# Scores of the two longest row blocks moved ahead of the product with v, in a three-stage attention pipeline on one core

## The reference

```python
def _L0_attn_ref(x, w_q, w_kv, w_dense):      # x: layer norm of (8, 512, 256)
    q = jnp.einsum('bsh,he->bse', x, w_q).reshape(b, sq, GROUPS, HPG, KVC)   # 4 groups, 4 heads each, width 128
    kv = jnp.einsum('bsh,he->bse', x, w_kv)
    k, v = jnp.split(kv, 2, axis=-1)           # one k and one v for each group
    ...
    scores = jnp.einsum('bqgpd,bkgd->bgqpk', q, k) * (SCALE / LAYER_INDEX)
    ...
    scores = jnp.where(causal[None, None, :, None, :], scores, -jnp.inf)
    probs = jax.nn.softmax(scores, axis=-1).astype(x.dtype)
    ctx = jnp.einsum('bgqpk,bkgd->bqgpd', probs, v).reshape(b, sq, HEADS * KVC)
    return jnp.einsum('bse,eh->bsh', ctx, w_dense)
...
x = x + 0.5 * ffn(layernorm(x)); x = x + attn(layernorm(x)); x = x + 0.5 * ffn(layernorm(x))
```

## Time and profile before

| | |
|---|---|
| time, 3 runs | 2637.43, 2638.76, 2639.93 us (median 2638.76) |
| the profiled execution | 2639.36 us, of which its span is 2637.5 us and 1.86 us lie around it |
| PE busy | 2536.8 us, 96% of the span |
| DVE busy | 2157.0 us, 82% |
| ACT, POOL busy | 946.0 us (36%), 910.4 us (35%) |
| one item of the attention, 984.50 to 1104.30 us | 119.80 us, PE busy 117.75, DVE 101.47, ACT 90.65, POOL 47.01, granted clock 1.00 |

### The profile page before, as it was taken

The page is one execution under the profiler, slowest core; times in us unless marked ns, Lnnn a source line. Parts: engine busy times, 40 slices in busy tenths (PEclk is TensorE's granted clock), DMA queues, the critical chain, the costliest instruction groups (busy, mean ns, idle before and its releaser), DMA issues. The chain is left out here.

```text
span 2637.5 us, 45987 instructions
## 1 busy us (share of the span) xinstructions
PE 2536.8 (96%) x14500; PEld 2341.1 (89%) x14500; DVE 2157.0 (82%) x6164; ACT 946.0 (36%) x2546; POOL 910.4 (35%) x1952
## 2 busy tenths in 40 slices
PE   6999999999996999999999999997999999999998
PEld 6999999999995889898888988896899999999997
DVE  6888888888886788888888888886888888888887
ACT  3111101111113677777777777774211011111100
POOL 4332333233224334343434343333423333332321
PEclk9999999999998999999999999998999999999999
DMA  6000000000001454554455455555100000000000
GB/s 192 9 1 1 1 1 1 1 1 1 1 27 56 81 91 91 89 89 84 91 91 88 83 93 88 89 90 121 51 1 9 9 1 9 9 9 1 9 9 9
DMA packets 378738, 117.30 MB, mean 44 GB/s; under 512 B 338560, under 2 KB 377472, under 8 KB 378496
## 3 DMA queue, kind: packets, MB, share of 16 engines
q1 hardware_dynamic: 378496, 114.36, 22.1%
HBM read 26.24 MB, written 4.19 MB: 12 GB/s over the span
## 5 line engine op out<-in xcount | busy, mean ns | idle before, releaser
L555 PE MATMUL ffn_ring<-ffn_mix_weights,ffn_yT 128*128 128x384 f32 x5760 | 1154.9, 341 | 8.1 <-DVE ffn_mix_weights L790 5.8
L555 PEld LDWEIGHTS ffn_ring<-ffn_mix_weights,ffn_yT 128*128 128x128 f32 x5760 | 1007.1, 189 | 58.5 <-DVE ffn_mix_sums L725 15.7
L727 DVE SCALAR_TENSOR_TENSOR ffn_mix_sums<-ffn_ring,ffn_w,ffn_mix_sums 128x384 f32<-128x384 f32 x896 | 550.4, 615 | 241.5 <-PE ffn_ring L555 224.8
L1579 POOL CAST attn_probsT<-attn_turned 128x1024 fp32r<-128x1024 f16 (+3 forms) x512 | 348.5, 723 | 508.1 <-DVE attn_probs L1444 496.9
L605 PE MATMUL ffn_ring<-ffn_out_weights,ffn_avT 128*128 128x512 f32 x1536 | 440.4, 397 | 7.0 <-POOL ffn_avT L1028 4.5
L1512 ACT ACTIVATE attn_exponentials<-attn_exponentials,attn_score_neg_max 128x512 f32<-128x512 f32 (+3 forms) x512 | 285.6, 558 | 169.8 <-DVE attn_score_neg_max L1427 169.6
L605 PEld LDWEIGHTS ffn_ring<-ffn_out_weights,ffn_avT 128*128 128x128 f32 x1536 | 281.2, 188 | 36.2 <-POOL ffn_avT L1028 5.7
L1273 PE MATMUL attn_ctx<-attn_probsT,attn_v 128*128 128x256 f32 (+2 forms) x1536 | 276.1, 329 | 14.9 <-issue 7.8
L1273 PEld LDWEIGHTS attn_ctx<-attn_probsT,attn_v 128*128 128x128 f32 x1536 | 242.1, 190 | 37.3 <-issue 9.3
L1444 DVE SCALAR_TENSOR_TENSOR attn_probs<-attn_exponentials,attn_prob_factor,attn_probs 128x512 f16<-128x512 f32 (+3 forms) x512 | 254.3, 558 | 22.0 <-ACT attn_probs L1521 21.3
L1521 ACT ACTIVATE attn_probs<-attn_exponentials,attn_prob_factor 128x512 f16<-128x512 f32 (+3 forms) x512 | 250.1, 552 | 27.5 <-DVE attn_prob_factor L1437 16.0
(11 more groups left out here) (141 smaller groups left out, 2858.8 us busy)
## 6 DMA issues: line engine op xcount, KB each, us to landing
ffn_mix_stage<-in_L_ffn_q_proj_dram SPq DMA_DIRECT2D x32, 128.0 KB, 2.5
ffn_mix_stage<-in_L_ffn_k_proj_dram SPq DMA_DIRECT2D x32, 128.0 KB, 2.5
ffn_mix_stage<-in_L_ffn_v_proj_dram SPq DMA_DIRECT2D x32, 128.0 KB, 2.9
ffn_out_stage<-in_L_ffn_o_proj_dram SPq DMA_DIRECT2D x16, 256.0 KB, 3.0
attn_turned<-attn_probs SPq DMA_TRANSPOSE x256, 4.0
out_dram<-x SPq DMA_DIRECT2D x8, 512.0 KB, 2.9
x<-in_L_attn_x_dram SPq DMA_DIRECT2D x7, 512.0 KB, 8.1
early_stage<-in_L_attn_w_q_dram SPq DMA_DIRECT2D x4, 512.0 KB, 5.3
```

Of the source, the lines that this page charges most:

```text
L555: last = pe.matmul(bank[:, 0:QKV], yT[:, t % 2, h, k * P:(k + 1) * P], mix_half(e, wh)[:, k], start=(n == 0), stop=(n == 3 * CK - 1))
L727: dve.scalar_tensor_tensor(into, bank[:, 0:QKV], w[:, t, e:e + 1], into, ALU.mult, ALU.add).then_inc(mix_done, 1)
L1579: pool.tensor_copy(cast(i), landed(n, i).rearrange("p (j h q) -> p j h q", h=HL, q=P)).then_inc(t_cast, 1)
```

## The change

Two moves, one on PE and one on DVE. On PE, `scores(now, 3)` and `scores(now, 2)` come ahead of `attend(last)` in a slot. On DVE, `score_max(now, 2)` comes ahead of `split_context(last)`. No instruction is added, removed or altered. The lists of ACT, POOL and SP are as they were.

```diff
@@ -1357,11 +1357,11 @@
-                if last:
-                    attend(last)
                 if now:
                     scores(now, 3)
                     scores(now, 2)
+                if last:
+                    attend(last)
                 place("B")
@@ -1472,10 +1472,10 @@
                 if now:
                     score_max(now, 3)
+                    score_max(now, 2)
                 if last:
                     split_context(last)
                 if now:
-                    score_max(now, 2)
                     score_max(now, 1)
                     score_max(now, 0)
```

## The result

| | before | changed |
|---|---|---|
| median (6 runs each) | 2638.79 us | 2659.93 us |
| lowest to highest | 2637.43 to 2640.27 | 2655.45 to 2662.16 |
| span of the profiled execution | 2637.5 us | 2657.4 us (its own time 2659.2) |
| PE busy | 2536.8 us | 2547.1 us |
| one item of the attention | 119.80 us | 122.68 us |

The ratio is 1.0077 (95% interval 1.0066 to 1.0088): the changed kernel is 0.8% slower, 21.1 us, against 21 us in the forecast. The spans differ by 19.9 us.

What follows compares the result with a forecast made beforehand. PE, 96% busy, was taken to bound the kernel, with about 2 us idle per item. Terms summed to +2.8 us per item: 16.6 for six middle items, +2.0 first, +2.4 last, together +21, hence 2660 us, range 2643 to 2676.

Steps and rivals of the forecast that it cites:

- Scores 3 wait for q: Plain slots: scores 3 wait for q's low half, making each 7.07 us; four take 28.3 against 27.0, +1.3 us per item.
- k of group 0: Projected last in slot 15; scores 3 of the next item's slot 0 wait out its whole split, +1.67 us per item.
- k in slots 7 and 11: Scores 3 of the next slot wait for k's low half and restart, 0.26 us each; +0.45 us per item.
- Slots 2 and 3: Scores 3 and 2 fill attend's wait for v, but DVE behind add_to_x delays k's low half: -0.3 us per item.
- Slot 14: The second z transpose's wait of 0.35 us for q's low half goes: -0.35 us per item.
- The DVE move: Maximum 2 ahead of split_context: ACT gets it earlier, filling only idle time; dense still starts unhindered; costs nothing, 0.2 us to spare.
- the forecast's aside: In the slot after the v slots, the wait for q hides a further wait, of dense for attend's low half.
- dense is not the bound: Rival judged: dense becomes the bound, waiting for attend's low half in v slots too; +16 us on top, 2676 us; chance 0.10.
- The granted clock: Rival: PE's idle gaps bring the clock down, attend and scores costing 3 us more per item; 2681 us; chance 0.04.
- No change: Rival: waits for q only replace those for the casts, gains and losses cancel within 5 us; 2641 us; chance 0.10.
- Faster: Rival: q's low half comes at least 0.5 us earlier, by 6.44 us into the slot; 2632 us; chance 0.08.
- the wait row for q: Sign of being right: PE scores waiting for DVE attn_qT, near 0.4 us each in some 30 to 40 slots.

Runs made afterwards that it cites:

- S = 9 to 14: Kernel before with both moves made only in slots 9 to 14, the light ones: 2648.79 us, ratio 1.0044.
- added DVE instruction: One more DVE sum into a scratch tile ahead of q's low half: 2686.84 us in the changed kernel, 2643.32 us in the kernel with the DVE move alone.
- Slot 0 alone: Kernel before with both moves made only in slot 0 of each item: 2649.4 us, ratio 1.004.
- Slot 3 alone: Kernel before with both moves made only in slot 3 of each item: 2629.47 us, ratio 0.9965.
- The earlier k: Changed kernel with slot 15's two projections of the next item, q and k, one place earlier: 2642.65 us, ratio 1.0013.

## Why the prediction was right, and where it was not

Counted in both traces from the start of slot 0 of an item to that of the next (of the last item, to the first attend behind it), the loss is spread over the items as the forecast had it:

| | forecast | measured |
|---|---|---|
| first item | +2.0 us | 129.22 - 127.46 = +1.8 |
| six middle items | +16.6 | 736.65 - 720.43 = +16.2 |
| last item | +2.4 | 117.88 - 115.83 = +2.1 |

Together that is 20.0 us, and the spans differ by 19.9. That the median fell within 0.1 us of the forecast is luck, since the changed kernel's own runs spread over 7 us.

*Scores 3 wait for q.* Right in place and size. Forecast 7.07 us for a plain slot and 28.3 for the four, measured 7.13 and 7.07 for slots 9 and 10 and 14.12 for 12 and 13, 28.3 in all. The light slots alone (S = 9 to 14) cost 9.3 us, and an added DVE instruction went through to PE in full in the plain slots.

*k of group 0.* Right: slot 15 went from 8.87 to 10.50 us, and slot 0, where the restart falls, from 7.20 to 7.27, together +1.70 where 1.67 was forecast. Slot 0 alone cost 10.75 us.

*k in slots 7 and 11.* Right: slot 7 went from 7.91 to 8.13 us where 0.26 was forecast, and slot 11 is 8.26 us where 8.01 + 0.2 was the sum. In both, scores 3 of the next slot start 0.10 us behind the end of k's low half.

*Slots 2 and 3.* Right in the sum: 1121.08 - 1104.53 = 16.55 us against 17.01, with 0.1 of restart behind it, where -0.3 was forecast. The reason given, that DVE is late with k's low half behind add_to_x, is borne out by the timeline of DVE, in which no row from the first of these two to the second has idle time in brackets:

```profile
1113.35 1.27 DVE L1459 TENSOR_TENSOR x<-x,attn_dense 128x512 f32<-128x512 f32 x2
...
1120.29 0.69 DVE L1412 TENSOR_TENSOR attn_kT<-attn_projections,attn_kT 128x512 fp32r<-128x512 f32 x1
```

No run takes add_to_x away, so its own share is not shown. Slot 3 alone, followed by an attend that covers k's split, keeps 9.2 us. In the changed kernel much of that goes to the wait for k (0.42 in slot 4's row).

*Slot 14.* Right in size: 1202.15 - 1194.66 = 7.49 us against 7.90, where -0.35 was forecast. It doesn't need both moves. The wait of the second z transpose is gone with either half alone, and slot 14 then lasts 7.66 us (PE half) or 7.39 (DVE half, as part of its 0.8 us per item).

*The DVE move.* This is the step that failed, though the number held. I wrote that maximum 2 earlier "only fills idle time" and costs nothing. It is worth 6.7 us alone and 14 us inside the change (2674.09 against 2659.93). Nor is it free for dense, which waits 0.3 us for attend's low half in slot 9. I had priced its direct neighbours, dense and exponential 2, and not followed the queue on ACT one step on: exponential 2, then the high half of q, then q's low half, which is what scores 3 wait for. The forecast was still right, and in this part by luck, because the 6.92 us that it was built on hold only with this move (7.03 in the changed kernel, with the restart of 0.10 in it that the sum books by itself; 7.16 without the move). I had read them from a slot in which attend came early, and assumed that they did not depend on where attend stands. On PE they don't; through DVE and ACT they do, and the second half of the change happens to undo that.

*The rivals.* Dense waits 2.8 us in all, in slot 9 of seven items and once in slot 10; slot 9 is the one that the forecast's aside named, and dense is not the bound. The granted clock stayed at 1.00 over the stretch from 1100 to 1222 us, with the idle 1.46 us in it. "No change" needed the wait for q at under half, and the four plain slots cost 1.3 us together, as forecast. "Faster" needed q's low half 0.5 us earlier, and DVE's 0.57 us of idle in front of maximum 1 shows why it couldn't be. Of the signs named ahead, the wait row for q has 22 entries of 0.33 us on average, and not 30 to 40 of 0.4; by the starts there are five such slots per item, and the view doesn't list them all.

Two misses among the experiments can be read from the traces. The earlier k gave 17.3 us and not 14.3: slot 15 became shorter by about 2.27 us and not by 2.05 in each of seven items, and slot 3 of the first item by 0.8, 16.5 us over the attention. Why slot 15 gives 0.2 us more than its two waits is not settled. The added instruction cost 26.9 us and not 31: the plain slots grew by 0.3 us and the slots 1, 5 and 6 by 0.25, but slots 7 and 11, which wait for k and not for q, by only 0.21 and 0.08 where 0.34 was expected. What is left in both lies within the spread of the changed kernel's own runs (2655.45 to 2662.16).

## What to carry to other kernels

A product whose inputs were ready long ago is cover: placed between the last split of an operand and the first use of it, it hides the latency of two engines. Moving it away costs, in each round, what nothing else covers of that latency, even with PE 96% busy: here about 0.3 us in a plain slot, 1.7 where k came last, and next to nothing in the slots with a v projection. Before moving a step up, look at when its newest operand is finished, counted from the start of the round, and at which engine that moment is tied to. And follow a moved step through every queue behind it: what stood behind maximum 2 on ACT was worth 14 us.

Where one round in sixteen has a real wait, change that round alone. Here the two moves, made only in slot 3, won 9 us; made in all slots, they lost 21.
